# Graph attention with one edge per partition: the queries spread by a one-hot product, one PSUM sum per 24 chunks, the output stage inside the loop

## The reference

```python
h = relu(layernorm(x)); x = x + L0(h, edges)      # two mean convolutions, rows normalised
h = relu(layernorm(x)); x = x + L1(h, edges)      # one mean convolution, log map / exp map
h = relu(layernorm(x)); x = x + L2(h, src, dst)   # three mean convolutions
h = relu(layernorm(x)); x = x + L3(h, src, dst)   # attention, 8 heads of 16

def L3(x, src, dst):
    Q, K, V = x @ Wq + bq, x @ Wk + bk, x @ Wv + bv
    score = exp(clip(sum(K[src] * Q[dst], per head) / 4, -5, 5))
    wV = segment_sum(V[src] * score, dst);  z = segment_sum(score, dst)
    h = layer_norm(x + wV / (z + 0.001), gamma1, beta1)
    return h + relu(layer_norm(h, gamma2, beta2) @ Wo + bo)
```

## Time and profile before

| | |
|---|---|
| median of 3 runs | 2767.84 us (2763.7 to 2769.82) |
| span of the profiled execution (its own time) | 2766.6 us |
| busy in the span: PE, PEld | 2011.8 us (73%), 1374.8 us (50%) |
| busy: DVE, ACT, POOL | 1445.3 us (52%), 919.2 us (33%), 1123.8 us (41%) |
| gathers, line 1049 | 816, 790.0 us busy, 476.6 us idle before them |
| granted TensorE clock, mean | 0.811 |
| mean DMA rate | 57 GB/s |

### The profile page before, as it was taken

One profiled execution on the slowest core, in us unless ns is written; L12 is line 12 of the kernel. 1 busy time (PEld: TensorE's weight loads), 2 busy tenths in 40 slices (PEclk: granted clock), 3 DMA queues, 4 the chain that ended last, 5 costly groups with the idle time before them and its releaser, 6 DMA issues. The chain is left out here.

```text
span 2766.6 us, 52529 instructions
## 1 busy us (share of the span) xinstructions
PE 2011.8 (73%) x10406; PEld 1374.8 (50%) x10407; DVE 1445.3 (52%) x4933; ACT 919.2 (33%) x2759; POOL 1123.8 (41%) x1567
## 2 busy tenths in 40 slices
PE   2666665799879999989376677766667667767745
PEld 0111111465436566655266576766557556756723
DVE  8888886433555533333334444444444444444577
ACT  3888885333553322222411111111111111111101
POOL 2000001322433300012566666666666666666546
PEclk9999999999999999999656765667676676676655
DMA  1000000101111111012322222232232222222311
GB/s 47 0 0 0 0 0 24 40 25 33 42 40 55 52 29 31 28 54 83 106 87 86 83 84 85 85 87 85 82 90 83 84 86 86 86 84 83 76 38 40
DMA packets 135327, 158.44 MB, mean 57 GB/s; under 512 B 23985, under 2 KB 107750, under 8 KB 135142
## 3 DMA queue, kind: packets, MB, share of 16 engines
q0 software_dynamic: 39168, 107.01, 13.6%
q1 hardware_dynamic: 96102, 50.80, 6.2%
HBM read 134.81 MB, written 22.90 MB: 57 GB/s over the span
## 5 line engine op out<-in xcount | busy, mean ns | idle before, releaser
L1049 POOL DMA_INDIRECT counts<-keys_values,index x816 | 790.0, 968 | 476.6 <-issue 226.6
L709 PE MATMUL z_bank<-y_parts,counts 128*128 128x384 bf16 x3750 | 674.4, 328 | 3.9 <-issue 3.9
L709 PEld LDWEIGHTS z_bank<-y_parts,counts 128*128 (+1 forms) x3750 | 369.1, 98 | 236.8 <-issue 14.4
L1121 PE MATMUL ao_bank<-masked,counts 128*128 128x64 f32 x1632 | 314.9, 356 | 181.7 <-DVE masked L1179 164.5
L1111 PE MATMUL as_bank<-counts,kT 128*128 x1632 | 312.2, 358 | 156.4 <-ACT kT L1075 86.0
L1111 PEld LDWEIGHTS as_bank<-counts,kT 128*128 128x128 f32 x1632 | 308.1, 281 | 173.4 <-issue 173.3
L1121 PEld LDWEIGHTS ao_bank<-masked,counts 128*128 128x128 f32 x1632 | 288.4, 265 | 197.8 <-DVE masked L1179 135.7
L440 PE MATMUL share_build<-right_build,left_build 128*128 128x300 bf16 x816 | 276.7, 443 | 128.6 <-DVE right_build L378 97.7
L1162 DVE TENSOR_SCALAR clipped<-as_bank 128x256 f32<-128x256 f32 x204 | 85.6, 420 | 392.4 <-remote 229.5
L1081 ACT ACTIVATE weight<-clipped 128x256 f32<-128x256 f32 x204 | 85.0, 417 | 585.0 <-DVE clipped L1162 420.1
L1075 ACT ACTIVATE kT<-at_bank 128x512 f32<-128x512 f32 x204 | 120.5, 590 | 450.6 <-remote 299.4
(11 more groups left out here) (148 smaller groups left out, 2170.1 us busy)
## 6 DMA issues: line engine op xcount, KB each, us to landing
counts<-keys_values,index POOLq DMA_INDIRECT x816
self_term<-s_out SPq DMA_DIRECT2D x150, 64.0 KB, 1.6
s_in<-self_term SPq DMA_DIRECT2D x150, 64.0 KB, 1.8
residual<-x_in SPq DMA_DIRECT2D x75, 64.0 KB, 1.6
x_in<-in_x SPq DMA_DIRECT2D x50, 64.0 KB, 1.8
x_in<-residual SPq DMA_DIRECT2D x50, 64.0 KB, 1.8
keys_values<-s_out SPq DMA_DIRECT2D x25, 128.0 KB, 1.7
attention_input<-h SPq DMA_DIRECT2D x25, 64.0 KB, 1.6
```

The lines of the kernel that those rows point to most:

```text
L709: ins = nc.tensor.matmul(z_bank[k.slot()][:, 0:YW], lhs, y3[(p - 1) % 2][:, s, :], start=s == 0, stop=s == NT - 1)
L1049: nc.gpsimd.indirect_dma_start(rows_kv[:, j, c, :], None, v.kv, bass.IndirectOffsetOnAxis(index[:, j, c:c + 1], 0)).then_inc(gathered[j], 16)
L1121: nc.tensor.matmul(o_bank[g2.slot()][:, c * W * H:(c + 1) * W * H], rows_kv[:, (j - 2) % GU, c, D:2 * D], masked[:, g2.slot(), c * W * H:( ...
```

## The change

The attention stage is written anew. An edge now stands on a partition from the gather on.

- Groups are 24 chunks (`GE` = 3072 edges, `NG` = 34), in 202 steps of four chunks. A group's nodes lie in a window of 128 that begins at the node of its first edge (`v.bases`). The build computes each edge's place in the window (`rel_rows`, `rel_cols`), stores both, and adds a check for gaps.
- Pass 6 makes untransposed queries, adds all biases on DVE (`biased`), and stores the scaled queries in three bf16 parts (`query_part` on ACT, `second` on DVE).
- Per group DVE makes the one-hot `spread` (3072 columns) from a row that a DMA broadcasts. Per step PE multiplies it with the window's queries (`q_bank`, three parts to each chunk), DVE multiplies with the keys (`prod`), makes the one-hot `pick`, sums `prod` per head, and multiplies the values with the weights of the step before (`msg`); ACT takes the exponential; PE adds `pick` x `msg` to one PSUM bank over the whole group, two steps later.
- A sum that belongs to the next window goes over by a product with `shift`.
- Division, the two norms, the product with `Wo` and the store of group g-1 and g-2 are done inside the loop, spread over its steps; powers become Ln and Exp on ACT. `finish` is not called on this path any more.
- POOL issues only gathers; a slot is given back by `msg_done`.

The core of the new loop:

```diff
+            dve.wait_ge(bases_in, 48)
+            chain.step(nc.vector.tensor_scalar(row_base[:, :], row_base[:, :], float(LASTBASE), None, ALU.min))
+            chain.step(nc.vector.tensor_scalar(col_base[:, :], col_base[:, :], float(LASTBASE), None, ALU.min))
+            chain.step(nc.vector.tensor_scalar(v.bases[:, :], base_row[:, :], float(LASTBASE), None, ALU.min))
+            nc.vector.tensor_tensor(row_rel[:, :, :], dst_rows[:, :, :], row_base[:, :].unsqueeze(2).to_broadcast([P, CR, P]),
+                                    ALU.subtract).then_inc(rel_ready, 1)
+            nc.vector.tensor_tensor(col_rel[:, :], dst_cols[:, :], col_base[:, :], ALU.subtract).then_inc(rel_ready, 1)
+            chain.step(nc.vector.tensor_tensor(gap[:, :], v.bases[:, LEAD + 1:LEAD + NG + 1], v.bases[:, LEAD:LEAD + NG], ALU.subtract))
+            chain.step(nc.vector.tensor_reduce(gap_flag[:, 0:1], gap[:, :], AX.X, ALU.max))
+            chain.step(nc.vector.tensor_scalar(gap_flag[:, 0:1], gap_flag[:, 0:1], float(P), None, ALU.is_gt))
+            chain.step(nc.vector.tensor_scalar(gap_flag[:, 1:2], v.bases[:, LEAD + NG - 1:LEAD + NG], float(LASTBASE), None, ALU.is_lt))
+            chain.step(nc.vector.tensor_tensor(gap_flag[:, 0:1], gap_flag[:, 0:1], gap_flag[:, 1:2], ALU.max))
+            dve.wait_ge(rel_ready, 2)
             dve.wait_ge(starts_in, 16)
...
-                    ins = nc.tensor.matmul(out_[:, 2 * D:3 * D], wq, hT[:, n.slot(), :], start=True, stop=True)
+                    ins = nc.tensor.matmul(out_[:, 2 * D:3 * D], hT[:, n.slot(), :], wq, start=True, stop=True)
...
+            def query_part(p, dt):
+
+                if p == 6:
+                    (dt + 1).count(act, qkv_ready)
+                    if by_edge:
+                        nth(ALL, p, dt - 1).count(act, y_ready)
+                    else:
+                        (dt - 2).landed(act, q_st)
+                    nc.scalar.activation(q_part[:, dt.slot(), 0:D], qkv[:, dt.slot(), 2 * D:3 * D], ACT.Copy,
+                                         scale=float(DH) ** -0.5).then_inc(part_ready, 1)
...
+            def biased(p, dt):
+
+                n = nth(ALL, p, dt)
+                (n + 1).count(dve, d_done)
+                (n - 2).landed(dve, s_st)
+                if by_edge:
+                    (dt - 2).landed(dve, q_st)
+                chain.step(nc.vector.tensor_tensor(qkv[:, dt.slot(), 0:2 * D], d_bank[n.slot()][:, 0:2 * D], bias[p % 2][:, :], ALU.add))
+                nc.vector.tensor_tensor(qkv[:, dt.slot(), 2 * D:3 * D], d_bank[n.slot()][:, 2 * D:3 * D], bq, ALU.add).then_inc(qkv_ready, 1)
...
+            def step(s, g, j):
+                if sub(s):
+                    (s + 1).count(pool, index_ready, held)
+                    (s - (RG - 1)).count(pool, msg_done, held)
...
+                if sub(s):
+                    (s + 1).count(act, clip_done)
+                    (s - 2).count(act, agg_done)
+                    nc.scalar.activation(msg[:, s.slot(3), :, D:TW], clipped[:, s.slot(), :].rearrange("p (c h) -> p c h", c=GC),
+                                         ACT.Exp).then_inc(exp_done, 1)
...
+            def step(s, g, j):
+                if sub(s):
+                    if j == 0:
+                        (g + 1).count(pe, spread_ready)
+                        g.landed(pe, q_ld)
+                    (s - 1).count(pe, prod_done)
+                    for c in range(GC):
+                        for i in range(PARTS):
+                            ins = nc.tensor.matmul(q_bank[s.slot()][:, c * P:c * P + P],
+                                                   spread[:, g.slot(), (j * GC + c) * P:(j * GC + c) * P + P],
+                                                   queries[:, g.slot(), i * D:i * D + D], start=i == 0, stop=i == PARTS - 1)
+                    ins.then_inc(q_done, 1)
+                s2 = s - 2
+                if sub(s2):
+                    ga = g if j >= 2 else g - 1
+                    if j == 2:
+                        (ga - 1).count(pe, total_ready)
+                    (s2 + 1).count(pe, msg_done)
+                    (s2 + 1).count(pe, pick_done)
+                    (s2 + 1).count(pe, exp_done)
+                    for c in range(GC):
+                        ins = nc.tensor.matmul(acc_bank[ga.slot()][:, 0:TW], pick[:, s2.slot(3), c, :], msg[:, s2.slot(3), c, :],
+                                               start=j == 2 and c == 0, stop=False)
+                    ins.then_inc(agg_done, 1)
+                g1, g2 = g - 1, g - 2
+                if j == 1 and group(g1):
+                    (g1 + 1).count(pe, shift_ready)
+                    g1.count(pe, total_ready)
+                    nc.tensor.matmul(acc_bank[g1.slot()][:, 0:TW], shift[:, g1.slot(), :], total[:, (g1 - 1).slot(), :],
+                                     start=False, stop=True).then_inc(acc_done, 1)
+                if j == 0 and group(g2):
+                    (g2 + 1).count(pe, n2_ready)
+                    g2.count(pe, n2T_ready)
+                    nc.tensor.transpose(t_bank[:, 0:P], n2[:, :], v.ident[:, :]).then_inc(t_done, 1)
+                if j == 1 and group(g2):
+                    (g2 + 1).count(pe, n2T_ready)
+                    g2.count(pe, res_ready)
...
+            def spread_queries(g):
+
+                g.landed(dve, wide_ld)
+                if g.c >= 2:
+                    dve.wait_ge(q_done, (g - 1).value(GS))
+                nc.vector.tensor_scalar(spread[:, g.slot(), :], rel_wide[:, g.slot(), :], v.lane[:, :], None,
+                                        ALU.is_equal).then_inc(spread_ready, 1)
...
+            def step(s, g, j):
+                s1 = s - 1
+                if sub(s):
+                    turn = (s.c // RG + 1) * 16 * GC
+                    dve.wait_ge(gathered[j], turn if s.k is None else s.k * (PAIR // RG * 16 * GC) + turn)
+                    (s + 1).count(dve, q_done)
+                    nc.vector.tensor_tensor(prod[:, :].rearrange("p (c d) -> p c d", c=GC), q_bank[s.slot()][:, :].rearrange("p (c d) -> p c d", c=GC),
+                                            rows_kv[:, j, :, 0:D], ALU.mult).then_inc(prod_done, 1)
+                    (s - 2).count(dve, agg_done)
+                    nc.vector.tensor_tensor(pick[:, s.slot(3), :, :], rel_cols[:, bass.ds(s.value(GC), GC)].unsqueeze(2).to_broadcast([P, GC, P]),
+                                            v.iota[:, :].unsqueeze(1).to_broadcast([P, GC, P]), ALU.is_equal).then_inc(pick_done, 1)
+                    (s + 1).count(dve, prod_done)
+                    nc.vector.tensor_reduce(score[:, s.slot(), :], prod[:, :].rearrange("p (n d) -> p n d", d=DH), AX.X,
+                                            ALU.add).then_inc(sum_done, 1)
+                if sub(s1):
+                    (s1 + 1).count(dve, exp_done)
+                    wide = msg[:, s1.slot(3), :, :]
+                    nc.vector.tensor_tensor(wide[:, :, 0:D].rearrange("p c (h d) -> p c h d", h=H),
+                                            rows_kv[:, (j - 1) % RG, :, D:2 * D].rearrange("p c (h d) -> p c h d", h=H),
+                                            wide[:, :, D:TW].unsqueeze(3).to_broadcast([P, GC, H, DH]), ALU.mult).then_inc(msg_done, 1)
+                if sub(s):
+                    (s + 1).count(dve, sum_done)
+                    nc.vector.tensor_scalar(clipped[:, s.slot(), :], score[:, s.slot(), :], -5.0, 5.0, ALU.max, ALU.min).then_inc(clip_done, 1)
+                g1, g2 = g - 1, g - 2
+                if j == 1 and group(g + 1):
+                    spread_queries(g + 1)
+                if j == 0 and group(g):
+                    shift_nodes(g)
+                if j == 3 and group(g1):
+                    attended(g1)
+                if j == 4 and group(g1):
+                    first_norm(g1)
+                if j == 5 and group(g1):
+                    second_norm(g1)
+                if j == 2 and group(g2):
+                    result(g2)
+
+            over_steps(step, chain, 2 * 15)
+            tail(step)
```

588 lines of the change are left out of this document (318 added, 270 removed).

## The result

| | before | after |
|---|---|---|
| median of 9 runs each, same chip | 2767.31 us (2763.70 to 2772.01) | 2780.98 us (2772.96 to 2785.28) |
| span of the profiled execution | 2766.6 us | 2781.1 us |
| first to last start of a gather | 1354.1 to 2618.5 | 1365.3 to 2731.2 |
| that is, for each gather | 1264.4 / 815 = 1.55 us | 1365.9 / 807 = 1.69 us |

A forecast was written before the change was run, and what follows sets the result against it. The slot round trip through PE was taken as the bound, POOL's gather pitch right behind. Block start 1363, first gather 1368, loop 1131 to 2499, end 2525 gave 2526 us, 8.7% less; own range 2430 to 2640.

The forecast's parts named there:

- This round trip: Old attention loop: a ring slot returns only after a chain three times through PE; two groups take 12.4 us, not 10.
- 808 gathers x 1.25 = 1010 us: New attention loop: POOL issues 202 steps of four gathers, each at its own pitch of 1.25 us.
- Build: Build stage: 3.8 us more DVE work, mostly taken by idle time behind it; +1 us (0 to 4).
- Pass 6: Biases and query splitting on DVE delay PE by 0.6 us a tile: 15 us (0 to 45).
- Start: Start of attention: first gather 5.0 us after the block's start instead of 8.7, at 1368 us.
- Port costs: New loop: gathers lose time to DVE's `pick`, `msg`, `spread` and small operations; 121 us in the loop's sum.
- first rival: No port cost: phases miss and DVE's small operations take nothing from gathers; 2405 us, chance 0.10.
- DVE: New loop: 2.95 us a step, 25.0 us a group, hidden under POOL's 33.3 with 8 us to spare.
- PE: New loop: at the low clock 4.0 us a step, under POOL's 5.0.
- ACT: New loop: none to four table loads a group, at most 5 us of 33, hidden.
- Tail: After the last gather start: landing, last step, norms, product and store; 26 us in place of 127.
- Third rival: `prod` waits for PE's `q_done` as `clipped` waited, 5.78 us per two steps; 2832 us, chance 0.15.

The follow-up runs named there:

- e3: Changed kernel with POOL gathering only two of the four chunks of each step: 2171.33 us, ratio 0.783 to the kernel before.
- the probe: Changed kernel with four stages of independent engine work ahead of attention, 48 indexed gathers in each of the first three: one execution, 3246.33 us.
- e2: Changed kernel without the two lower bf16 query parts, four query products a step for twelve: 2742.91 us, ratio 0.988 to the kernel before.
- e4: Changed kernel with the attention loop written out on every engine: 2721.01 us, ratio 0.980 to the kernel before.
- e10: Changed kernel, POOL waiting after each step's first gather for the landing of the step before: 2778.57 us, ratio 1.003 to the kernel before.
- e17: Changed kernel with a 1024-column fill on POOL after every four gathers, on the fifth chip: 2600.08 us; kernel before there 2543.59.

## Why the prediction was wrong

**The step that failed** is the second one of "What bounds the kernel now": "This round trip is the bound; right behind it lies POOL's own pitch." The waits of POOL were put down to this chain, so the largest term, "808 gathers x 1.25 = 1010 us", leaves them out. The numbers of the earlier trace rows were right, 1.54 us a gather with 225 us of waits. The cause was not: the chain is what the change removes, and the waits were the slowness beside the gathers, which it keeps. Measured in that term's place: 1366 us, 1.69 us a gather. e3 (the same steps and half the gathers) shows that nothing else holds the loop at this pace, and the probe shows that the engines crawl when none needs another. Its sign lay in the releasers of the earlier trace rows: of POOL's waits 207.7 us were "remote" and only 31.3 named PE, and of DVE's 214.8 us before line 1154 only 28.7. The one wait of the earlier trace rows that I followed did lie behind work of PE; I took it for all of them.

- *Why more than before, 1.69 against 1.55.* Not settled. e2 (fewer products) and e4 (no loop) each brought 0.05 to 0.07 us a gather back. The rest was not taken apart.
- *Build:* predicted +1 us. The first product of line 709 (759 after) starts at 526.5 us against 527.4: nothing.
- *Pass 6:* predicted 0.6 us a tile, 15 us. From the first to the last `x_in` (24 tiles) 133.0 us became 144.3: +11.3, the right mechanism and size.
- *Start:* first gather predicted at 1368 us, came at 1365.3.
- *Port costs* (+121 us): gathers have a mean of 960 ns and a median of 946, so 808 x 0.014 = 11 us, as the first rival had it. But that goes for a DVE that stands still half of the time. In e10, where DVE keeps step, the mean is 1072 ns: 102 us in all, and of the 227 gathers of over 1.05 us 193 start while `pick` runs. There the rule of the Trainium skill that I leaned on ("SBUF — State Buffer", "Who interferes with whom") shows, and the term was about the right size; in the changed kernel it shows only in single gathers, up to 1.72 us. The upper bound for `spread` was misread: 3200 columns of line 1146 take 3.0 us, not 3.1, which moves nothing.
- *DVE* (2.95 us a step, 25.0 a group, 8 to spare): the operations sum to 2.94; with half the gathers a group took 22.7 us, so the 25.0 was a little high and DVE hidden as predicted. *PE* (up to 4.0 us a step): 585 us / 202 = 2.9. *ACT* (none to four table loads a group): four, 1283 ns each, and hidden.
- *Tail* (26 us): 49.9 us from the last start of a gather. One long gap (14.9 us between two `prod`) still lies in it; the rest of the difference was not followed.
- *Third rival* (2832 us; DVE before `prod` with PE as the releaser). Its sign came, its condition was met (2.6 us of wait a step; measured 571 / 174 = 3.3), and so did its mechanism as far as it went: the wait lies in how PE's results reach DVE, the increments of `q_done`. The forecast gave it 0.15. What it had wrong is the source: this is no price of PE's results, but of the gathers beside them. In e10 DVE waits 3.5 us in 700 for PE, with half the gathers 20.1. It came out 51 us above the measured time.

Terms together: start -2.7, loop +235, tail +24 make the 256 us between 2525 and the span of 2781.1.

What stays open: by what means indexed gathers slow the others, why the fifth chip is free of it, and how the changed kernel does there without fills. One rival was not tried. Every time here comes from an execution whose events were recorded, and where the engines crawl most of the gathers' own increments are missing from the trace (on record: 1990 of 12928 in the changed kernel, 7214 in e10, 12903 in e17). So the recording may have a part in the slowness, or only suffer from it.

## What to carry to other kernels

Before a wait is put down to a chain, check that the chain has work in it: when the last record of the producer and the landing lie well before the wait's end, the wait is something else, be it only the signal, and can survive a change of the chain. An average pace of gathers above their own pitch is a measurement, not slack to be won: price the new loop at the old pace as one bound, here 808 x 1.55 = 1252 us in place of 1131, which alone would have put the sum at 2646 us. If many engines stand while one issues, leave out half of what that one does, first of all; that run separated in one step what three on the chain could not.
